# GpSimd issues the last batch's token stack, and the fourth batch's norm parts stand at other products of the first expert stage

## The reference

```
sa, ca, ga, sb, cb, gb = modulation(silu(c) @ wmod)
h = layernorm(x) * (1 + ca) + sa
x = x + ga * (causal attention with rotary, 16 heads of 8)(h)
h = layernorm(x) * (1 + cb) + sb
t = (h @ Wm + bm) as 8 slices of 16 per token
w = softmax(t @ expert_emb); the two largest of 16 are kept
eo = gelu(t @ W1[e] + b1[e]) @ W2[e] + b2[e]    for each of the 16 experts
x = x + gb * ((sum of the two chosen, weighted) @ Wo + bo)
```

## Time and profile before

| | |
|---|---|
| median of 3 runs | 380.98 us |
| the profiled execution | 380.57 us |
| its span | 378.6 us |
| TensorE busy | 333.6 us (88%) |
| VectorE busy | 276.9 us (73%) |
| ScalarE busy | 259.9 us (69%) |
| GpSimd busy | 158.3 us (42%) |
| chain of waits: TensorE, VectorE, DMA | 48%, 25%, 10% |
| of the DMA's share: `dense<-tp` | 4% |
| `tstack<-tp`, 18 copies, issue to landing | 4.8 us median |
| `dense<-tp`, 6 copies, issue to landing | 10.0 us median |

### The profile page before, as it was taken

The page is one execution under the profiler, slowest core; times in us unless marked ns, Lnnn a source line. Parts: engine busy times, 40 slices in busy tenths (PEclk is TensorE's granted clock), DMA queues, the critical chain, the costliest instruction groups (busy, mean ns, idle before and its releaser), DMA issues.

```text
span 378.6 us, 7197 instructions
## 1 busy us (share of the span) xinstructions
PE 333.6 (88%) x2636; PEld 152.6 (40%) x2636; DVE 276.9 (73%) x569; ACT 259.9 (69%) x282; POOL 158.3 (42%) x189
## 2 busy tenths in 40 slices
PE   3759698988899899799999899989998889789996
PEld 3414254545555334233655344435553323141123
DVE  4879968788899688879699677864589467953334
ACT  8581373445489888674488988855679797959980
POOL 6249299801306343852209154932140146232500
PEclk9968879999999999999999999999999999999999
DMA  7335031400017255510136255530060457625551
GB/s 265 106 72 84 18 72 32 66 3 3 4 44 103 70 139 146 175 30 0 32 75 87 75 138 135 141 54 6 28 86 0 120 137 139 121 63 134 151 139 31
DMA packets 27115, 31.46 MB, mean 83 GB/s; under 512 B 6780, under 2 KB 17788, under 8 KB 27068
## 3 DMA queue, kind: packets, MB, share of 16 engines
q1 hardware_dynamic: 23372, 28.50, 32.6%
q0 software_dynamic: 3456, 2.39, 3.1%
q10 hardware_dynamic: 252, 0.11, 0.2%
HBM read 3.50 MB, written 1.05 MB: 12 GB/s over the span
## 4 chain that ended last, share of the span: by engine, by line
PE 48%; DVE 25%; DMA 10%; issue 7%; ACT 4%; SPq 4%; POOL 2%; DVEq 0%; ACTq 0%; POOLq 0%
PE big L1360 16%; PE misc L1360 16%; PE acc L1360 14%; DVE mx L1080 7%; DMA dense<-tp 4%; ACT ring L818 3%; DMA gm<-wT 2%; PE misc L1382 2%; DMA dense<-nm 2%; SPq L448 2%; DMA block<-qk_turned 1%; SPq L501 1%; DVE gm L1207 1%; DVE second L1172 1%; DVE xn L1014 1%
## 5 line engine op out<-in xcount | busy, mean ns | idle before, releaser
L818 ACT ACTIVATE ring<-big 128x1024 f32<-128x1024 f32 (+1 forms) x201 | 195.3, 1021 | 72.2 <-PE big L1360 71.3
L1080 DVE TENSOR_REDUCE mx<-misc 128x1 f32<-128x512 f32 (+7 forms) x155 | 87.4, 588 | 27.2 <-PE misc L1360 25.3
L1360 PE MATMUL acc<-ring,cb 128*32 128x512 f32 x512 | 67.7, 604 | 3.1 <-ACT ring L818 1.6
L1360 PE MATMUL big<-tstack,w1s 128*128 128x512 bf16 x192 | 55.0, 381 | 4.2 <-ACT ring L818 3.8
L1360 PE MATMUL big<-dense,block 128*128 128x512 bf16 (+7 forms) x256 | 51.9, 308 | 0.8 <-DMA dense<-nm 0.3
L1360 PE MATMUL misc<-dense,block 128*128 128x320 bf16 (+7 forms) x170 | 43.4, 315 | 8.6 <-DVE mx L1080 7.9
L1207 DVE SCALAR_TENSOR_TENSOR gm<-acc,cb,gm 128x512 f32<-128x512 f32 (+1 forms) x41 | 30.0, 734 | 27.3 <-PE acc L1360 19.4
L455 POOL DMA_DIRECT2D block<-qk_turned x66 | 39.3, 601 | 2.3 <-DMA tstack<-tp 2.0
L700 POOL TENSOR_TENSOR gm<-osb,gm 128x512 f32<-128x512 f32 x12 | 15.8, 1315 | 57.4 <-ACT osb L867 42.6
L1360 PEld LDWEIGHTS misc<-dense,block 128*128 128x128 bf16 x170 | 20.7, 149 | 47.1 <-DVE mx L1080 38.0
L1360 PEld LDWEIGHTS big<-dense,block 128*128 128x128 bf16 x256 | 28.8, 149 | 24.6 <-ACT ring L818 9.7
(11 more groups left out here) (169 smaller groups left out, 470.8 us busy)
## 6 DMA issues: line engine op xcount, KB each, us to landing
gm<-wT SPq DMA_DIRECT2D x64, 256.0 KB
dense<-qk SPq DMA_DIRECT2D x42, 64.0 KB
tstack<-tp SPq DMA_DIRECT2D x18, 128.0 KB, 4.8
block<-qk_turned POOLq DMA_DIRECT2D x66, 32.0 KB, 3.1
xs<-in_x SPq DMA_DIRECT2D x4, 256.0 KB, 7.6
out<-lg SPq DMA_DIRECT2D x3, 256.0 KB, 2.5
dense<-tp SPq DMA_DIRECT2D x6, 128.0 KB, 10.0
dense<-nm SPq DMA_DIRECT2D x45, 4.0 KB, 2.1
```

Of the source, the lines that this page charges most:

```text
L818: act.activation(dst, src, func, scale=scale).then_inc(s["ring_read"], 1)
L1080: dve.tensor_reduce(mx[:, g, k:k + n, blk], src, AX.X, ALU.max).then_inc(s["misc_read"], 1)
L1360: return pe.matmul(dst, lhsT, rhs, start=start, stop=stop)
```

## The change

It has two parts that share no code.

The last batch's token stack is issued by GpSimd, after its product n = 7 and the two sums behind it, with a semaphore of its own (`tail_stacked`), for which TensorE waits in the last batch. `stack_tokens` now takes the engine. SyncE no longer waits for the tokens between the two sets of spreads.

In the first expert stage the norm parts move. VectorE: the last two statistics from n = 5 to 4, the variance from 7 to 5, root and first normalisation from 12 to 11, the second and third normalisation from 13 and 14 to 13 together; the first statistics (3) and the fourth normalisation (15) stay. GpSimd: `rsqrt` from behind n = 11 to behind n = 7.

```diff
--- before.py
+++ after.py
@@ -366,7 +366,7 @@
             "qk_ready", "qk_turned", "k_dense_stacked", "q_block0_stacked", "q_block1_stacked", "q_dense_stacked", "k_block_stacked", "nm_ready",
             "shift_stacked0", "shift_stacked1", "tp_ready", "t_stacked", "ex_ready", "w_ready",
             "gm_ready0", "gm_ready1", "biased", "stored", "ln_link", "rope_link", "shift_link", "norm_link", "split_link",
-            "route_link", "tail_ones", "nmr_ready", "nm_rounded")}
+            "route_link", "tail_ones", "nmr_ready", "nm_rounded", "tail_stacked")}
         w_spread = [ctx.enter_context(nc.semaphore(f"w_spread{k}")) for k in range(GMS)]
         shift_stacked = [s["shift_stacked0"], s["shift_stacked1"]]
 
@@ -447,6 +447,15 @@
                     r = 3 * a + j
                     eng.dma_start(q_dense_of[b][r:r + 1, GP * g:GP * g + GP, :],
                                   nm[:, g, j, BLK * a:BLK * a + BLK]).then_inc(shift_stacked[g], 16)
+
+        def stack_tokens(eng, b, done="t_stacked"):
+
+            last = -1
+            for c, j in enumerate(PARTS_L):
+                if j != last:
+                    wait_part(eng, "split_link", SPLIT_LINKS, 0, b, j)
+                    last = j
+                eng.dma_start(tstack_of[b][FD * c:FD * c + FD, :, :], tp[j][:, :]).then_inc(s[done], 16)
 
         def block_diagonal(eng, dst, c, a, j, at, stack):
 
@@ -515,15 +524,6 @@
             def stack_shift(b, groups=range(NG)):
                 for g in groups:
                     shift_rows(sp, b, g, range(1 if b == g == 0 else 2))
-
-            def stack_tokens(b):
-
-                last = -1
-                for c, j in enumerate(PARTS_L):
-                    if j != last:
-                        wait_part(sp, "split_link", SPLIT_LINKS, 0, b, j)
-                        last = j
-                    sp.dma_start(tstack_of[b][FD * c:FD * c + FD, :, :], tp[j][:, :]).then_inc(s["t_stacked"], 16)
 
             def spread_weights(here, slots=range(GMS)):
 
@@ -559,17 +559,15 @@
             for b in range(NB - 2):
                 here = ("loop", b)
                 stack_k(b + 2)
-                stack_tokens(b)
+                stack_tokens(sp, b)
                 stack_q_block(b + 2)
                 spread_weights(here)
                 stack_q(b + 2, b)
                 stack_shift(b + 2)
                 store(here)
             here, tail = ("late", NB - 2), ("tail", NB - 1)
-            stack_tokens(NB - 2)
+            stack_tokens(sp, NB - 2)
             spread_weights(here)
-            sp.wait_ge(s["tail_ones"], 1)
-            stack_tokens(NB - 1)
             wait_filled(sp, here, "cb0")
             spread_weights(tail, range(GMS // 2))
             wait_filled(sp, here, "cb1")
@@ -760,14 +758,19 @@
                 add_bias(here)
                 stack_q(b + 2)
                 stack_k(b + 2, b)
-                experts_out(b, K_BLOCKS, {9: lambda: shift_rest(b + 2), 11: lambda: rsqrt(2 * b + 4, 0) if b + 3 < NB else None})
+                experts_out(b, K_BLOCKS, {7: lambda: rsqrt(2 * b + 4, 0) if b + 3 < NB else None, 9: lambda: shift_rest(b + 2)})
             here = ("late", NB - 2)
             fold_experts(here)
             rsqrt(2 * NB - 2, 1)
             wait_read(pool, here, "lg")
             fold_out(NB - 1, here)
             add_bias(here)
-            experts_out(NB - 2, between={5: lambda: rsqrt(2 * NB - 1, 1)})
+
+            def tail_tokens():
+                pool.wait_ge(s["tail_ones"], 1)
+                stack_tokens(pool, NB - 1, "tail_stacked")
+
+            experts_out(NB - 2, between={5: lambda: rsqrt(2 * NB - 1, 1), 7: tail_tokens})
             fold_experts(("last", NB - 1))
             add_bias(("tail", NB - 1))
             pool.wait_ge(s["x1b_ready"], NB)
@@ -1263,9 +1266,12 @@
                     root(n, 0, norm_link)
                     normal(src, 0, 0)
 
-                return {3: first_tiles, 5: last_tiles, 7: lambda: variance(0, norm_link), 12: begin,
-                        13: lambda: normal(src, 0, 1), 14: lambda: normal(src, 0, 2),
-                        15: lambda: normal(src, 0, 3).then_inc(s["xn_ready"], 1)}
+                def middle():
+                    for t in (1, 2):
+                        normal(src, 0, t)
+
+                return {3: first_tiles, 4: last_tiles, 5: lambda: variance(0, norm_link), 11: begin,
+                        13: middle, 15: lambda: normal(src, 0, 3).then_inc(s["xn_ready"], 1)}
 
             for k in range(GMS):
                 dve.sem_inc(w_spread[k], 16)
@@ -1595,7 +1601,10 @@
             def wait_tokens(b):
                 pe.wait_ge(s["w1_ready"], 1)
                 pe.wait_ge(s["tokens_one"], 1)
-                pe.wait_ge(s["t_stacked"], 16 * NC * (b + 1) + CREDIT["t_stacked"])
+                if b < NB - 1:
+                    pe.wait_ge(s["t_stacked"], 16 * NC * (b + 1) + CREDIT["t_stacked"])
+                else:
+                    pe.wait_ge(s["tail_stacked"], 16 * NC)
 
             def experts(here, phase, sums_read, ahead=False, next_sums=None, begun=0, between={}, before_fo=(), cb0_at=CB0_AT):
 
```

## The result

The changed kernel takes 383.25 us (median of 11 runs, 382.83 to 384.49), the kernel before 380.75 beside it (11 runs, 379.52 to 383.1): a ratio of 1.007, 95% interval 1.0053 to 1.0087. It is slower by 2.5 us. I had predicted 380.7, no measurable change. The profiled execution took 384.3 us, its span 382.4, with a mean granted clock of 0.969; before it was 380.57, 378.6 and 0.977.

The account below looks back on a forecast made before the run. VectorE's gapless tail routing and GpSimd's last product, not the stack's landing, were taken to bound the end. Terms +0.8 and −1.1 gave −0.3 us: 380.57 to 380.3, plus 0.41 for the median, 380.7; range 379.0 to 383.5.

Parts of the forecast that it names:

- What bounds the kernel: Tail: the stack's landing exposes at most 1.45 us of TensorE wait; with nothing delayed, removing it gains only 0.3 us.
- Part one, the issue cost: Tail: six stack issues on GpSimd at 0.6 us each, filling 316.75 to 320.4.
- The landing: Tail: the last stack copy, on GpSimd's queue, lands at 326 to 329; anything before 332.7 is the same.
- Part one, the lock: Tail: delayed GpSimd work blocks VectorE's two-input operations, VectorE 1.45 us later; part one's net term +0.8 us.
- 1.1 or more as a sign: Tail: L1168, L1171 and L1172 would each take 1.1 us or more, instead of 1.02, 0.93 and 0.69.
- Part two: First expert stage: moved norm parts avoid standing beside GpSimd, −1.1 us; ends −2.0 and 0.
- The issue cost goes by rows: Tail, slower: issues cost up to 2.35 us each; 383 at 1.7 us, 386.9 at 2.35; chance 0.2.
- The lock costs nothing more: Tail, faster: GpSimd's late work falls between VectorE's two-input operations, gaining 0.3 us; 379.6 down to 378.7; chance 0.25.
- The norm parts cost the same: First expert stage: norm parts gain 0 at their new places, leaving +0.8; 381.8; chance 0.15.
- the 0.5 that I had allowed: Tail: VectorE's casts and GpSimd's issues might hold each other up, 0.5 us at most.
- my chance for slower, 0.2: Whole kernel: slower than 382.9 us, through issues over about 1.6 us or smaller overruns of both parts together.

Follow-up runs that it names:

- stack_at11: Changed kernel with GpSimd's six stack issues behind its product n = 11 instead of n = 7; 378.93 us, 0.9951 of the kernel before.
- norm_only: Kernel before with only the norm parts moved, SyncE still issuing the stack; 378.8 us, 0.9952 of the kernel before.
- fill: Changed kernel, but SyncE issues the stack and GpSimd does 12 memsets in place of the issues; 381.22 us, 1.0008.
- fill13: Changed kernel, but SyncE issues the stack and GpSimd does 13 memsets in place of the issues; 381.89 us, 1.0023.
- fill_meet: Changed kernel, but SyncE issues the stack and GpSimd does 13 memsets and a small one (128x4) instead; 381.69 us, 1.0017.
- five_small: Changed kernel with five stack issues on GpSimd, one on SyncE, and a 128x4 memset with its wait before product n = 9; 380.12 us, 0.9979.
- gap: Changed kernel with a wait on GpSimd between its product n = 9 and the first sum behind it; 381.78 us, 1.003.
- five: Changed kernel with five stack issues on GpSimd and the sixth on SyncE; 382.99 us, 1.006.
- warm: Changed kernel with 14 extra TensorE products in its 4.33 us wait for VectorE's product n = 10; 381.48 us, 1.0018.
- after_again: Changed kernel unaltered, run again beside the other experiments; 383.44 us, 1.0072.
- after_small: Changed kernel with a 128x4 memset and its wait on GpSimd between the sixth issue and product n = 9; 379.38 us, 0.997.

## Why the prediction was wrong

**What bounds the kernel**: right in effect. The stack's landing was worth next to nothing. `stack_at11` and `norm_only`, with waits of 1.00 and 1.31 us for it, take the same time as each other, and I had put the whole gain at 0.3.

**Part one, the issue cost**: right, 0.55 us against 0.6. **The landing**: wrong and without consequence. I said 326 to 329, from copies of 32 KB that landed in 4.3 us; the last landed at 333.6, or 334.8 in the tail's own time, where before it was 333.95. Another queue did not bring it in earlier. The core's DMA engines were 0.87 busy from 316 to 320 us and 0.99 from 320 to 324, so the spreads' traffic is the likely reason, but no run takes it away. TensorE reached the stack at 336.89.

**Part one, the lock**: this step failed, in its form as well as in its size. I wrote that L1168 stands until the product's end and ends at 322.15, with the first sum behind it. It stood behind the product and the first sum, and ended at 323.69 (322.54, with the 1.15 us of part two added back). For n = 11 I wrote that it falls beside operations that do not meet it; it met L1172, as that came later too, 0.94 us. The operation between these two, L1171 in the earlier trace rows and L1174 now, took 0.92 us, no more than before, though I had named 1.1 or more as a sign. VectorE was late by 3.0 us where I had 1.45. The hand-over that I assumed does take place, in five kernels of the table (`fill`, `fill13`, `fill_meet`, `five_small`, `gap`), where an operation with a wait stands just ahead of the product or a wait just behind it; with transfers directly ahead of the product it did not, in `five` and in the changed kernel.

**A term that was missing**: the clock. I took every matmul at the length that it has in the trace of before. The delay made TensorE idle for 4.33 us, and the half clock behind it, over one and a half to three groups, cost some 2 us of the time (1.96 by the medians of `warm` and `after_again`).

**Part two**: the mechanism right, the size low: 1.9 us by the medians against 1.1, 1.35 in the stage itself by the profiled runs. The stretch of L1025 went whole (0.97 us), where I had counted 0.5. Taken apart by the starts of VectorE's products, each counted from the stage's first: n = 6 comes 0.32 us later (I had 0.4), n = 8 has then gained 2.25 (2.0), n = 10 loses 0.24, which I had counted as nothing and which has `rpow`, 1.03 us, newly ahead of GpSimd's n = 9, n = 12 loses 0.85 (0.7), and from there to `yT` 0.51 us are gained (0.2). That is 1.35; the further half microsecond of the medians no row places.

Put into the sum: −0.3 as predicted, +1.55 for the lock, +1.96 for the clock, −0.8 for part two, is +2.4; measured +2.5. The last two come from medians, the lock from a trace, so the agreement to 0.1 is partly luck.

**The rivals.** *The issue cost goes by rows* gave the slower side, for a reason that is false; no issue of the stack took over 0.70 us in any trace. *The lock costs nothing more*, 379.6 down to 378.7, is what happens with a place that is 0.2 us later (`after_small`, 379.38) or behind n = 11 (378.93), but not in the kernel as it is. *The norm parts cost the same* is false. Beside the issues VectorE's casts take 0.43 us as before, and the median issue 0.53. The first issue, though, begun 0.15 us before a cast, took 0.69 us and ended 0.11 us behind the cast's end, in the changed kernel and alike in every trace with the issues at this place; in `stack_at11`, with no cast beside it, the first took 0.61. So what the Trainium skill names ("SBUF — State Buffer", The "DVE blocks DMA" trap) is worth at most 0.16 us here, within the 0.5 that I had allowed; whether that 0.16 is the trap, no run shows. My range ended at 383.5 and held the result by luck: its upper end came from dear issues, and my chance for slower, 0.2, rested on that wrong mechanism.

**Shown**: that part one is the loss, that the meeting of GpSimd's late work with VectorE makes it (the same six issues cost nothing behind n = 11, and 0.6 us against `norm_only` with the small memset behind them), that about 2 us of it is the clock. **Open**: why GpSimd keeps VectorE standing through two operations when transfers were issued directly before, and hands over when a small operation with its wait stands between. The page of the profile calls GpSimd's spans rough, and a difference of 0.01 us in them says little; that in `gap` and in the changed kernel the pass stood behind a product recorded as begun 0.02 and 0.01 us after it may mean that the product had begun before its record does. No run shows that.

The version to keep is `norm_only`, 378.8 us, 0.5% below the kernel before; `stack_at11`, 378.93, cannot be told from it and changes more.

## What to carry to other kernels

Before work is moved ahead of other operations on GpSimd, lay the delayed ones beside VectorE's operations with two SBUF inputs: the price is not in the moved work but in whom the delayed work meets. One small memset with its wait, 0.2 us of GpSimd's time, made 4 us here (383.44 against 379.38); how much of that is the shift and how much what stands ahead of the product, these runs do not separate. When a delay lengthens a wait of TensorE, as here from 1.34 us to 2.8 and more, take the work behind it at both clock levels; products into a free bank during the wait, 14 or 8 of them here, kept the clock up. Where a wait at the end is hidden by another engine's chain, as the stack's was, taking it away is not worth a risk.
